# Recurrent part: one difference and three clamps on ScalarE in place of three VectorE arguments, and another order of the projections

## The reference, cut to what matters

```
h = layernorm(x); hh = h shifted by one token
k = (h*tmk + hh*(1-tmk)) @ Wk.T        # keys
v = (h*tmv + hh*(1-tmv)) @ Wv.T        # values
sr = sigmoid((h*tmr + hh*(1-tmr)) @ Wr.T)   # receptance
w = -exp(time_decay); u = time_first
for each token:                        # carry aa, bb, pp
    qq = max(pp, u + kk)
    out = (exp(pp-qq)*aa + exp(u+kk-qq)*vv) / (exp(pp-qq)*bb + exp(u+kk-qq))
    qq2 = max(pp + w, kk)
    aa, bb, pp = exp(pp+w-qq2)*aa + exp(kk-qq2)*vv, exp(pp+w-qq2)*bb + exp(kk-qq2), qq2
x = x + (sr*out) @ Wo.T
h = layernorm(x); the channel part: sigmoid(xr @ Wcr.T) * (relu(xk @ Wck.T)**2 @ Wcv.T), added to x
```

## Time and profile before

| | |
|---|---|
| median of 3 runs | 1838.99 us (1836.97 to 1839.28) |
| profiled execution | 1839.21 us, span 1837.5 us, mean granted TensorE clock 0.982 |
| busy over the span | TensorE 1736.6 us (95%), VectorE 1242.6 us (68%), ScalarE 977.0 us (53%) |
| recurrent part | about the first 705 us of the span; from keys to keys a step lasts 38.6 to 41.5 us |

### The profile page before, as it was taken

The page is one execution under the profiler, slowest core; times in us unless marked ns, Lnnn a source line. Parts: engine busy times, 40 slices in busy tenths (PEclk is TensorE's granted clock), DMA queues, the critical chain, the costliest instruction groups (busy, mean ns, idle before and its releaser), DMA issues.

```text
span 1837.5 us, 27225 instructions
## 1 busy us (share of the span) xinstructions
PE 1736.6 (95%) x10508; PEld 1520.3 (83%) x10508; DVE 1242.6 (68%) x1918; ACT 977.0 (53%) x1505; POOL 3.6 (0%) x26
## 2 busy tenths in 40 slices
PE   3599999999999998998999999999999999999997
PEld 1378888778888788888899889998999989999896
DVE  7999999999999855888554445444454544445446
ACT  4688898898989773444533333333333332333323
POOL 0000000000000000000000000000000000000000
PEclk9799999999999998999999999999999999999999
DMA  4000010001000002111111010000011001120001
GB/s 143 1 25 17 12 47 18 7 8 62 1 12 29 0 30 89 44 55 45 55 35 35 1 35 35 34 33 2 34 34 34 11 23 34 34 74 0 1 1 41
DMA packets 34702, 56.59 MB, mean 31 GB/s; under 512 B 3030, under 2 KB 20412, under 8 KB 33596
## 3 DMA queue, kind: packets, MB, share of 16 engines
q1 hardware_dynamic: 34620, 55.47, 9.3%
HBM read 51.79 MB, written 3.67 MB: 30 GB/s over the span
## 4 chain that ended last, share of the span: by engine, by line
PE 70%; DVE 24%; ACT 3%; issue 2%; DMA 0%; SPq 0%; ACTq 0%; DVEq 0%
PE fbank L1935 33%; PE fbank L1957 17%; PE pair L839 5%; PE pair L799 4%; PE pair L824 3%; DVE kfl L421 2%; PE proj L1429 2%; PE pair L809 2%; DVE st L268 2%; DVE aa L370 1%; DVE bb L366 1%; DVE pp L352 1%; PE qbanks L1465 1%; PE pair L789 1%; DVE x L409 1%
## 5 line engine op out<-in xcount | busy, mean ns | idle before, releaser
L1757 DVE TENSOR_TENSOR hf<-sil,fbank 128x512 f32<-128x512 f32 (+1 forms) x256 | 158.8, 620 | 479.2 <-PE fbank L1935 407.5
L1862 ACT ACTIVATE sil<-fbank 128x512 f32<-128x512 f32 (+1 forms) x256 | 139.2, 544 | 615.1 <-PE fbank L1935 615.1
L1935 PE MATMUL fbank<-xh,wh 128*128 128x512 f32 (+1 forms) x1024 | 289.8, 364 | 1.2 <-ACT sil L1862 1.2
L1935 PE MATMUL fbank<-xl,wh 128*128 128x512 f32 (+1 forms) x1024 | 289.0, 363 | 0.0
L1935 PE MATMUL fbank<-xh,wl 128*128 128x512 f32 (+1 forms) x1024 | 288.9, 363 | 0.0
L1957 PE MATMUL fbank<-wl,hh 128*128 128x256 f32 x896 | 250.3, 279 | 0.0
L1957 PE MATMUL fbank<-wh,hh 128*128 128x256 f32 x896 | 250.2, 279 | 0.0
L1957 PE MATMUL fbank<-wh,hl 128*128 128x256 f32 x896 | 250.1, 279 | 0.0
L1935 PEld LDWEIGHTS fbank<-xl,wh 128*128 128x128 f32 x1024 | 184.6, 189 | 30.8
L1935 PEld LDWEIGHTS fbank<-xh,wl 128*128 128x128 f32 x1024 | 184.4, 189 | 30.4
L1935 PEld LDWEIGHTS fbank<-xh,wh 128*128 128x128 f32 x1024 | 180.5, 189 | 27.8 <-ACT sil L1862 1.6
(11 more groups left out here) (239 smaller groups left out, 3109.6 us busy)
## 6 DMA issues: line engine op xcount, KB each, us to landing
raw<-in_w_gate SPq DMA_DIRECT2D x16, 512.0 KB, 3.8
raw<-in_w_up SPq DMA_DIRECT2D x16, 512.0 KB, 4.7
raw<-in_w_down SPq DMA_DIRECT2D x16, 512.0 KB, 5.7
raw<-in_w_ck SPq DMA_DIRECT2D x4, 1024.0 KB, 4.8
raw<-in_w_cv SPq DMA_DIRECT2D x4, 1024.0 KB, 4.8
raw<-in_ctx_t SPq DMA_DIRECT2D x4, 750.0 KB, 5.9
ct<-in_ctx_t SPq DMA_DIRECT2D x4, 750.0 KB, 4.9
x<-in_x SPq DMA_DIRECT2D x4, 448.0 KB, 6.9
```

The costliest lines, as they stand in the source:

```text
L1757: dve.tensor_tensor(hf[i][:, 0:w], sil[i][:, 0:w], banks(e, t, f)[1][:, 0:w], ALU.mult).then_inc(hf_ready, 1)
L1862: act.activation(sil[f % 2][:, 0:w], banks(e, t, f)[0][:, 0:w], ACT.Silu).then_inc(sil_ready, 1)
L1935: ins = pe.matmul(banks(e, t, f)[k][:, 0:w], m[h][:, o:o + P], a[:, b, columns(c)], start=i == 0, stop=i == 3 * CB - 1)
```

## The change

VectorE writes one difference, dp = pp(t-1) - k(t), and nothing else. With it w' = exp(time_decay) = -w: e1b = exp(-relu(w' - dp)), e2b = exp(-relu(dp + w)), and eu = exp(24 - relu(dp + 24 - u)), so each of the three is, on ScalarE, two Relu instructions of a half (the bias is a value for each channel), then one Exp over the whole tile. Two columns are added to the small parameters, `we` and `mostu`, with one more small VectorE instruction at the very start. From unit 2 on the projections come in the order keys, receptance, (channel gate of unit s), values; VectorE mixes in the same order; ScalarE takes the values out of their bank behind the second table load rather than ahead of the first. `place(m, name)` counts the semaphore values accordingly.

```diff
-        KVR = (1, 2, 0)
+        BANKS = {"k": 1, "v": 2, "r": 0}
+        def place(m, name):
+            return ("kvr" if m < 2 else "krv").index(name)
...
-                for name, mu in zip(("k", "v", "r"), ("tmk", "tmv", "tmr")):
+                for name in sorted("kvr", key=lambda name: place(m, name)):
...
-                du = rw[m % 2]
                 after(n)
-                dve.tensor_tensor(tokens(dp), at(pp, 0), at(pp, 1), ALU.subtract).then_inc(arg_ready, 1)
-                dve.tensor_tensor(tokens(dk), at(kp, 1), at(pp, 1), ALU.subtract).then_inc(arg_ready, 1)
-                for b in range(CB):
-                    dve.scalar_tensor_tensor(du[:, b], kp[:, b, :, 1:T1], param(m, b, "u"),
-                                             pp[:, b, :, 0:T], ALU.add, ALU.subtract).then_inc(arg_ready, 1)
+                dve.tensor_tensor(tokens(dp), at(pp, 0), at(kp, 1), ALU.subtract).then_inc(arg_ready, 1)
...
             def wkv_exp(m, what):
-                act.wait_ge(arg_ready, 4 * m + (what + 1 if what < 2 else 4))
+                def over(out, name, scale):
+                    for b in range(CB):
+                        act.activation(out[:, b], dp[:, b], ACT.Relu, bias=param(m, b, name), scale=scale)\
+                            .then_inc(side_ready, 1)
+                per = 3 * CB
                 if what == 0:
-                    for b in range(CB):
-                        act.activation(e1b[:, b, :, 1:T1], dp[:, b], ACT.Exp, bias=param(m, b, "w"))\
-                            .then_inc(exp_ready, 1)
+                    act.wait_ge(arg_ready, 1 * m + 1)
+                    t = e1b[:, :, :, 1:T1]
+                    over(t, "we", -1.0)
+                    act.wait_ge(side_ready, per * m + CB)
+                    act.activation(t, t, ACT.Exp, scale=-1.0).then_inc(exp_ready, 1)
                 elif what == 1:
-                    act.activation(e2b[:, :, :, 1:T1], dk[:], ACT.Exp).then_inc(exp_ready, 1)
+                    t = e2b[:, :, :, 1:T1]
+                    over(t, "w", 1.0)
+                    act.wait_ge(side_ready, per * m + 2 * CB)
+                    act.activation(t, t, ACT.Exp, scale=-1.0).then_inc(exp_ready, 1)
                 else:
-                    act.activation(eu[:], rw[m % 2][:], ACT.Relu, bias=most[:], scale=-1.0).then_inc(side_ready, 1)
-                    act.wait_ge(side_ready, m + 1)
+                    over(eu, "mostu", 1.0)
+                    act.wait_ge(side_ready, per * (m + 1))
                     act.activation(eu[:], eu[:], ACT.Exp, bias=most[:], scale=-1.0).then_inc(exp_ready, 1)
...
# ScalarE's step
-                if valid(s + 2):
-                    if s + 2:
-                        act.wait_ge(num_ready, s + 2)
-                    out(s + 2, 1, v[:], v_out)
                 if valid(s + 2) or valid(s):
                     act.preload_act_table_set(EXP_TANH)
                 if valid(s + 2):
-                    out(s + 2, 2, th[:], th_ready, ACT.Tanh, 0.5)
+                    act.wait_ge(num_ready, s + 2)
+                    out(s + 2, "r", th[:], th_ready, ACT.Tanh, 0.5)
...
                 if valid(s + 3):
                     rsqrt0(1, s + 3)
+                if valid(s + 2):
+                    out(s + 2, "v", v[:], v_out)
                 if valid(s):
                     hidden(s, 0)
...
# TensorE's step
-                    project(m, 0, wk, mixed["k"], "k")
-                    project(m, 1, wv, mixed["v"], "v")
+                    project(m, "k", wk)
+                    if m < 2:
+                        project(m, "v", wv)
...
-                    project(m, 2, wr, mixed["r"], "r")
+                    project(m, "r", wr)
...
                     tokens_out(pair[3], mixed["cr"], wcr, mix2_ready, 4 * m, CB).then_inc(cr_done, 1)
+                    if valid(m + 2):
+                        project(m + 2, "v", wv)
```

More of the change, by code:

```diff
@@ L25 @@
 FT = F // P
-NAMES = ["ln1w", "ln1b", "tmk", "tmv", "tmr", "td", "u", "ln2w", "ln2b", "cmk", "cmr", "w", "pmk", "pmr"]
+NAMES = ["ln1w", "ln1b", "tmk", "tmv", "tmr", "td", "u", "ln2w", "ln2b", "cmk", "cmr", "w", "we", "mostu", "pmk", "pmr"]
 PRM = {n: i for i, n in enumerate(NAMES)}
@@ L320, in mix1 @@
                 after(difference(m))
-                for name, mu in zip(("k", "v", "r"), ("tmk", "tmv", "tmr")):
+                for name in sorted("kvr", key=lambda name: place(m, name)):
                     for b in range(CB):
-                        dve.scalar_tensor_tensor(mixed[name][:, b], diff[:, b], param(m, b, mu),
+                        dve.scalar_tensor_tensor(mixed[name][:, b], diff[:, b], param(m, b, "tm" + name),
                                                  h[1][:, b, :, 0:T], ALU.mult, ALU.add).then_inc(mix1_ready, 1)
@@ L352, in wkv_arguments @@
                 n = did(dve.tensor_tensor_scan(flat(pp), flat(decay), flat(kp), 0.0, ALU.add, ALU.max))
-                du = rw[m % 2]
                 after(n)
-                dve.tensor_tensor(tokens(dp), at(pp, 0), at(pp, 1), ALU.subtract).then_inc(arg_ready, 1)
-                dve.tensor_tensor(tokens(dk), at(kp, 1), at(pp, 1), ALU.subtract).then_inc(arg_ready, 1)
-                for b in range(CB):
-                    dve.scalar_tensor_tensor(du[:, b], kp[:, b, :, 1:T1], param(m, b, "u"),
-                                             pp[:, b, :, 0:T], ALU.add, ALU.subtract).then_inc(arg_ready, 1)
+                dve.tensor_tensor(tokens(dp), at(pp, 0), at(kp, 1), ALU.subtract).then_inc(arg_ready, 1)
             def wkv_sums(m):
-                dve.wait_ge(exp_ready, 4 * m + 3)
+                dve.wait_ge(exp_ready, 3 * m + 2)
                 did(dve.tensor_tensor_scan(flat(bb), flat(e1b), flat(e2b), 0.0, ALU.mult, ALU.add))
@@ L372, in wkv_denominator @@
             def wkv_denominator(m):
-                dve.wait_ge(exp_ready, 4 * m + 4)
+                dve.wait_ge(exp_ready, 3 * m + 3)
                 dve.tensor_tensor(tokens(dp), tokens(eu), at(bb, 0), ALU.add).then_inc(den_ready, 1)
@@ L465, in vector @@
             pw = PRM["w"]
-            dve.tensor_scalar(prm[:, :, :, pw:pw + 1], prm[:, :, :, pw:pw + 1], -1.0, None, ALU.mult).then_inc(w_ready, 1)
+            pe, pu, pm = PRM["we"], PRM["u"], PRM["mostu"]
+            dve.tensor_scalar(prm[:, :, :, pw:pw + 1], prm[:, :, :, pe:pe + 1], -1.0, None, ALU.mult).then_inc(w_ready, 1)
+            dve.tensor_scalar(prm[:, :, :, pm:pm + 1], prm[:, :, :, pu:pu + 1], -1.0, MOST, ALU.mult, ALU.add)\
+                .then_inc(w_ready, 1)
             for name in ("ln1w", "ln2w"):
@@ L473, in vector @@
                     .then_inc(w_ready, 1)
-            dve.wait_ge(w_ready, 5)
+            dve.wait_ge(w_ready, 6)
             input_stats(0)
@@ L612, in normalise, with out @@
                 ins.then_inc(xn_ready[k], 1)
-            def out(m, which, dst, done, func=ACT.Copy, scale=1.0):
-                act.wait_ge(kvr_done, 3 * m + which + 1)
-                act.activation(dst, pair[KVR[which]][:, :, 0:G * T].rearrange("p b (g t) -> p b g t", t=T), func,
+            def out(m, name, dst, done, func=ACT.Copy, scale=1.0):
+                act.wait_ge(kvr_done, 3 * m + place(m, name) + 1)
+                act.activation(dst, pair[BANKS[name]][:, :, 0:G * T].rearrange("p b (g t) -> p b g t", t=T), func,
                                scale=scale).then_inc(done, 1)
@@ L684, in scalar @@
             act.preload_act_table_set(LN_EXP)
-            act.activation(prm[:, :, :, PRM["w"]:PRM["w"] + 1], prm[:, :, :, PRM["td"]:PRM["td"] + 1],
+            act.activation(prm[:, :, :, PRM["we"]:PRM["we"] + 1], prm[:, :, :, PRM["td"]:PRM["td"] + 1],
                            ACT.Exp).then_inc(wexp_done, 1)
-            act.wait_ge(w_ready, 5)
+            act.wait_ge(w_ready, 6)
             rsqrt0(0, 0)
@@ L695, in scalar @@
             rsqrt0(0, 2)
-            out(0, 0, kp[:, :, :, 1:T1], k_out)
+            out(0, "k", kp[:, :, :, 1:T1], k_out)
             rsqrt0(1, 1)
-            out(0, 1, v[:], v_out)
+            out(0, "v", v[:], v_out)
             wkv_exp(0, 0)
@@ L704, in scalar @@
             act.preload_act_table_set(EXP_TANH)
-            out(0, 2, th[:], th_ready, ACT.Tanh, 0.5)
+            out(0, "r", th[:], th_ready, ACT.Tanh, 0.5)
             act.preload_act_table_set(LN_EXP)
@@ L709, in scalar @@
             rsqrt0(0, 3)
-            out(1, 0, kp[:, :, :, 1:T1], k_out)
+            out(1, "k", kp[:, :, :, 1:T1], k_out)
             act.wait_ge(num_ready, 1)
-            out(1, 1, v[:], v_out)
+            out(1, "v", v[:], v_out)
             act.preload_act_table_set(EXP_TANH)
-            out(1, 2, th[:], th_ready, ACT.Tanh, 0.5)
+            out(1, "r", th[:], th_ready, ACT.Tanh, 0.5)
             act.preload_act_table_set(LN_EXP)
@@ L734, in scalar @@
                 if valid(s + 2):
-                    out(s + 2, 0, kp[:, :, :, 1:T1], k_out)
+                    out(s + 2, "k", kp[:, :, :, 1:T1], k_out)
                 if valid(s):
```

(8 more changed lines are left out.)

## The result

The changed kernel takes 1858.47 us (1858.06 to 1860.28, four runs) against 1837.98 us (1836.64 to 1839.28, four runs): ratio 1.0112, interval 1.0101 to 1.0124, so 20.5 us slower. The forecast was 1858, with 1848 to 1868. The profiled executions took 1858.06 and 1839.21 us, with spans of 1856.3 and 1837.5 us.

A forecast was written before the change was run, and what follows sets the result against it. It took ScalarE's leg from hidden(s, 0) to y as closing the step; 14.9 (13 steps) + 1.6 + 0.3 + 0.1 (filling, start) + 2.1 (step 13) = +19.0 on 1839.2, so 1858 us, range 1848 to 1868.

The forecast's parts named there:

- The closing chain: Plain step: ScalarE from hidden(s, 0) to y, VectorE to kfl[3], TensorE's last quarter to the next keys; 38.60 us before.
- The price of the exponents: ScalarE between hidden(s, 0) and y: two half Relus plus a whole Exp each, +2.55 us (bounds +2.2 and +5).
- The rule for Relu: Skill's advice to put relu on VectorE; by its ratio the kernel would end near 1915; set aside for the trace.
- The start of the leg: hidden(s, 0) on ScalarE starts 14.94 us behind the keys rather than 15.48, with 1.5 us of waiting ahead.
- The steps: Keys to keys: 40.6 us in plain steps, 41.15 in steps 0, 4, 8, 12; +14.9 us over 13 steps.
- Filling and step 13: Pipeline filling later by 1.6, 0.3 and 0.1 us; step 13, where bb waits for e2b, by 2.1 us.
- the leg through bb: From hidden(s, 0) through the exponents to VectorE's scan of bb and on to yy, reached at 34.8 us.
- the leg through y: ScalarE's work from hidden(s, 0) to the end of y, reached at 35.05 us behind the keys.
- (a): Rival: VectorE is the bound and cutting its arguments pays, 1828 us; chance 0.10.
- (b): Rival: the reorder pays for the Relus by using ScalarE's 2.54 us idle whole, 1838 to 1842 us; chance 0.07.
- (c): Rival: slower, Exps pay a drain behind Relus or half Relus cost more, +12 us, 1870 us; chance 0.08.
- (d): Rival: hidden layer's quarter 2 waits for the values' bank, needing ScalarE 3.7 us late; chance counted inside (c).

The follow-up runs named there:

- e3: Changed kernel with the Relu instructions of e1b and e2b left out, so both are 1 and the output is wrong: 1822.69 us (0.9915 of the kernel before).
- e4: Changed kernel with VectorE's two removed arguments done again for nobody, in their old place: 1858.62 us (1.0114 of the kernel before).
- e6: Changed kernel with ScalarE's normalise(1, s+3) moved ahead of hidden(s, 0), VectorE's small norm instructions also earlier, one more TensorE Relu wait: 1872.65 us.
- e7: Changed kernel with e6's early norm, and VectorE also writing the old dk so that e2b is one Exp again: 1849.42 us.
- e9: Kernel before, in new order; units 2, 4, 6 and so on use dp, plus dk for a one-Exp e2b; others the old three arguments: 1832.93 us.
- e1: Changed kernel's arguments alone, with projections and the values' evacuation in the old order: 1861.81 us (1.0132 of the kernel before).
- e2: New order alone, with the old three arguments by VectorE and the old exponents: 1837.81 us (0.9998 of the kernel before).

## Why the prediction was right

*The closing chain.* ScalarE's leg from `hidden(s, 0)` to y, then kfl[3], then the last quarter. That ScalarE's leg closes the step is shown by e3 (take 2.5 us from it and the steps fall to TensorE's floor) and e4 (VectorE's 35 us beside it cost nothing). The two runs don't tell the way through y from the one through bb, which hangs on the same instructions of ScalarE.

*The price of the exponents.* +2.55 was said; e1b and e2b take 4.22 instead of 1.96 (473.40 to 477.62), eu 2.20 instead of 2.01: +2.45. A pair of half Relus is 1.22, as the half Exps were. Relu passes and whole Exps stand 0.03 apart as said.

*The rule for Relu.* The Trainium skill's "ScalarE: Activation LUTs", section "Rules for kernel authors", puts relu on VectorE, which is up to about three times as fast per element in bf16. I had set it aside because a whole Relu on ScalarE (1.03) and a whole subtraction on VectorE (1.08) are equal in fp32. That was the wrong row: the subtraction reads two tiles, and a Relu reads one. The changed kernel's trace has a VectorE instruction that, like the half Relu, reads one tile and a value for each channel (behind the first bar: us in all, mean ns of one):

```profile
L352 DVE TENSOR_SCALAR decay<-reset,prm 128x452 f32<-128x452 f32 x8 | 3.2, 447 | 0.0
L657 ACT ACTIVATE e1b<-dp,prm 128x448 f32<-128x448 f32 x32 | 19.5, 656 | 3.7 <-DVE dp L358 3.7
```

So for a half tile in fp32 VectorE takes 0.45 us and ScalarE 0.66. No run put the Relus on VectorE, where the waits of 2.22 and 2.46 us would have had some room for them; whether that order of work pays is open. The forecast didn't hang on it, as its sum used ScalarE's own rows.

*The start of the leg.* 14.94 was said, it is 15.12, with 1.51 us idle ahead of it as said; the first quarter of the hidden layer ends 15.08 behind the keys in the trace, a little later than I had worked out from starts. This 0.18 too little and the exponents' 0.10 too much nearly cancel. The gate's Tanh kept 0.46 of its 2.54 us. In steps 4, 8, 12 it is 15.39 (15.5 said).

*The steps.* 40.6 said and 40.65 measured in plain steps, 41.15 and 40.93 in steps 4, 8, 12. Step 0, for which 41.15 was said too, takes 41.95; its first 2.5 us still ran at a granted clock of 0.5, which the sum had left out. Over all 13 it is 618.44 - 87.75 = 530.69, said 530.0, before 515.13.

*Filling and step 13.* +2.0 said, 87.75 - 85.70 = 2.05 measured; the first scan of bb comes 1.91 later (42.42 against 40.51), said 1.7. bb in step 13 comes 19.84 later than before (640.68 against 620.84), of which 2.2 are the step's own, said 2.1. Of these 19.8 the end of the span keeps 18.8: at the last quarter of the channel output it is 19.2 (719.6 instead of 700.4), and the rest comes back in the parts behind it. Behind the keys of step 13 the same 7606 matmuls keep TensorE busy 1195.4 us instead of 1197.4, and ahead of the last 10 us the clock was at 0.5 for 20.4 us instead of 27.3; that this is the cause was not tested.

*The sum.* It started from the profiled execution, 1839.2, and added 19.0; the two profiled executions are 18.85 apart. The medians are 20.5 apart, and their interval is some 18.6 to 22.8 us.

*What was only luck.* I had the leg through bb and the leg through y at 34.8 and 35.05 and left it at "just before". That they nearly tie was harmless for this change, which lengthens both alike, and it decided e6 and e7. A third way, through eu, ties with y: eu ends at 487.42, VectorE's dp, dk and rw follow from 487.45 to 490.67, and y ends at 490.63. The output projection's wait for a Relu (0.74 us, said 0.8) is one more leg, and it has 1.01 us of room, the wait for kfl[3] that is left behind it (said 1.2).

*The rivals.* (a) is refuted by e4 for the changed kernel; before the change VectorE did hold the longer steps (e3, e9), and the exponents ate more than its cut gave; (b) by e1 and e2 (the order gives 0.36 of the 2.45 us), (c) by the rows above; (d) too: v leaves its bank 13.6 us behind the keys and nothing waits for it.

## What to carry to other kernels

In a pipeline of engines with queues in order, ask which chain closes the step before asking who is fullest: the engine with 12% free was the one that could bear nothing. Moving work pays only where the giver's leg is the longest in that step and the taker's isn't; steps differ, and the same edit that loses 20 us everywhere gains 4 to 5 us in half of its size and in every other step, with the new order (e9). And before taking an instruction out of the longest leg, write down the second and third: here they were 0 and 0.3 us behind.

## What the runs showed of the hardware

Two ScalarE instructions of which the second reads what the first wrote stand 0.03 us apart, where independent ones overlap by 0.09 to 0.1 (471.56 to 473.40 in step 9 has both): a chain of small passes costs some 0.12 us for each link beside the passes. A table load takes 1.28 us and the next instruction starts 0.02 behind it (the load at 466.21, the small one at 467.51).

For a tile of 128x448 in fp32 with a value for each channel, a VectorE instruction that reads one tile took 0.45 us (128x452) and a ScalarE instruction 0.66.

The clock granted to TensorE fell to 0.5 (1.2 GHz) for 3.4 us in six of e6's steps, each time about the end of an idle time of 2.2 or 3.1 us, and didn't fall in a seventh with an idle time of 2.2 us. Between two steps that are alike otherwise, the fall cost TensorE 1.4 us of busy time and the step 0.7.
